# Carrying a super-tile's last projection and its sum of squares into the next super-tile, in a recurrent state-space layer

## The chip, the cores and the metric

The kernel runs on one core of one Trainium2 chip. The metric is the device time of one launch in microseconds (us); lower is better. The engines are TensorE (PE in the profile, with its weight loads as PEld), VectorE (DVE), ScalarE (ACT), GpSimd (POOL) and SyncE (SP), which here only issues DMAs.

## The reference, cut to what matters

```python
x = u                                       # (4, 1024, 128), 4096 tokens
xn = layernorm(x)
proj = xn @ in_proj_w.T                     # z, x, B, C, dt, theta, lambda; 32 heads of 64
B, C = rope(rms(B) + B_bias), rope(rms(C) + C_bias)      # per head, angles = cumsum(theta)
h = a_t * h + g_t * Bx_t + b_t * Bx_(t-1)   # state per head, scanned over the tokens
y = einsum(h, C) + D * x
y = y * silu(z)                             # 2048 features a token
y = y * rsqrt(mean(y * y) + eps) * norm_w
out = u + (y @ out_proj_w.T) * silu(fp8_ffn(xn))
```

The mean of squares runs over all 2048 features of a token, so it is known only when all heads are done. As it is one factor a token, the kernel projects the unscaled y and multiplies the result with the factor afterwards.

## The kernel before, in words

A first part (`prepare`) normalises the tokens, makes decays and tables, and stores them in DRAM; it lasts to about 137 us. The second part (`units`) is the rest. It works in 8 super-tiles `t` of 512 tokens (4 chunks of 128), and in each of them in 8 groups `q` of 4 heads (two pairs). One (t, q) is called a unit here; there are 64. A sequence has 1024 tokens, so `begins(t)` is true of even t and `ends(t)` of odd t; a super-tile that ends a sequence leaves out the last state update.

Each engine runs a list written out by hand, in which work for unit q, q+1 and q+2 is interleaved; semaphores hold the engines together, and `at(per, t, k)` is the count that a wait asks for.

- DVE in a unit: two products `part` a rotation (`rotation`, L1220), of B and C with sines and cosines, eight a unit and one of them ahead of `angles` (L1194); the state updates (L1269, L1279), `x_scaled` (L1204, from the two banks R[0] and R[1]), `scores` (M, L1238), `yT` = y * silu(z) (L1311), `b_decayed` (bw, L1230).
- POOL in a unit: `sums` (L1412) adds two `part` into `rot`, four times; `c_decayed` (ce, L1421); the running sum `sqa` of the squares of yT (L1465, in q = 0 L1458).
- ACT in a unit: `rounding`, `decays` (E, L1353), silu of z (sz, L1388), `sines`, `squares` (sq, L1358).
- PE in a unit: `angles`, the state products (L1111), `exponents` (L1051, into bank Dp), `scores` (L1062), `x_by_token` (L1036, two halves, into R[0] and R[1]), `project` (L1076, the output projection of the unit before, 16 matmuls into the bank Op, which one matmul of zeros opens, L1071), z (L1137), y (L1143, L1149, L1159, banks Yp[0] and Yp[1]), then B by token (L1042) and the first exponents and scores of the next unit.

At the end of a super-tile PE runs the projection of the last unit (`project(t, 7, range(CS))`, L1175) and then the sums of squares (L1180: 8 small matmuls of `sqa` with ones into Dp), and only then the next super-tile's angles and state products. DVE takes the sums in `norm_start` (L1244) of the next super-tile's unit 0, between its first rotation product and its `angles`; ACT takes the root (L1364), DVE the reciprocal (`norm_seeded`, L1249), POOL refines it in four small operations (`norm_refined`, L1427 to L1433, between `c_decayed` and the second of the four `sums`), ACT scales Op into `so` (`normalised`, L1372, four pieces, last in its unit 0), and POOL multiplies with the gate and adds the residual at the end of unit 1 (`finished`). PE waits for `ssq_taken`, which `norm_start` raises, before its state products of unit 0, and for `acc_done`, which `normalised` raises, before the first projection of the new super-tile in unit 1.

Of the kernel before, what the change touches and what calls it, by code (L numbers as in the profile page):

```python
# [27 lines left out]
P = 128  # L28
# [5 lines left out]
CS = 4  # L34
# [788 lines left out]
def units(nc, K, u, scratch, cum_stored, out):  # L823

    xn_d, tc_d, bc_d, cum_d, cumt_d, gate_d, ecum_d = scratch
    with ExitStack() as ctx:
# [196 lines left out]
        def _(pe):  # L1023
# [43 lines left out]
            def project(t, q, chunks):  # L1067

                if q == 0 and chunks[0] == 0:
                    pe.wait_ge(acc_done, at(1, t, 0))  # L1070
                    nc.tensor.matmul(Op[:], K["zeros_bf"][0:MASK_ROWS, :], K["cum"][0:MASK_ROWS, 0, 0, :], start=True, stop=False, skip_group_check=True)  # L1071
                pe.wait_ge(yt_ready, at(T2, t, 2 * q + 2))
                for c in chunks:
                    k = slice(c * P, c * P + P)
                    for p in range(2):
                        last = nc.tensor.matmul(Op[:, k], yT[:, p, k], K["w_o"][:, (2 * q + p) * P:(2 * q + p + 1) * P],  # L1076
                                                start=False, stop=q == NQ - 1 and c == CS - 1 and p == 1,
                                                skip_group_check=True)
                if chunks[-1] == CS - 1:
                    last.then_inc(out_ready, 1)  # L1080


            pe.wait_ge(xn_loaded, 16)
# [10 lines left out]
            for t in range(NS):  # L1094
                for q in range(NQ):
# [6 lines left out]
                    if live(t, q + 2):  # L1102
                        angles(t, q + 2)
                    if q == 0:
                        pe.wait_ge(ssq_taken, at(1, t, 0))

                    pe.wait_ge(bw_ready, at(T2, t, 2 * q + 2))
# [9 lines left out]
                    scores(t, q, 1)  # L1117
                    exponents(t, q, 3)
                    if live(t, q + 1):
                        if q == NQ - 1:  # L1120
                            pe.wait_ge(xn_loaded, (t + 2) * 16)
                        if live(t, q + 2):
                            pe.wait_ge(turned, at(T1, t, q + 3))
                        x_by_token(t, q + 1, 0)
                    if q > 0:
                        project(t, q - 1, (0, 1))
                    pe.wait_ge(hch, at(T8, t, 8 * q + 8))
                    if live(t, q + 1):
                        x_by_token(t, q + 1, 1)
                    if q > 0:  # L1130
                        project(t, q - 1, (2, 3))
                    for p in range(2):
# [4 lines left out]
                        nc.tensor.matmul(R[p][:], w, xns[:, t % 2, :], start=True, stop=True).then_inc(z_ready, 1)  # L1137

                    for p in range(2):
                        pe.wait_ge(m_ready, at(T4, t, 4 * q + 2 * p + 2))  # L1140
# [33 lines left out]
                    exponents(t, q + 1, 1)  # L1174
                project(t, NQ - 1, range(CS))  # L1175

                pe.wait_ge(sqa_ready, at(T2, t, T2))
                pe.wait_ge(e_ready, at(T4, t, T4 + 2 if live(t, NQ) else T4))
                for c in range(CS):
                    last = nc.tensor.matmul(Dp[:, c:c + 1], sqa[:, c * P:c * P + P], K["ones"][:, 0:1],  # L1180
                                            start=True, stop=True)
                last.then_inc(ssq_ready, 1)

        @block.vector
        def _(dve):
# [54 lines left out]
            def norm_start(t):  # L1240

                dve.wait_ge(ssq_ready, at(1, t, 1))
                dve.wait_ge(norm_ready, t)
                nc.vector.tensor_scalar(nrm[:, 0, :], Dp[:, 0:CS], 1.0 / DI, EPS, ALU.mult, ALU.add).then_inc(ssq_taken, 1)  # L1244

# [15 lines left out]
            for t in range(NS):  # L1261
# [21 lines left out]
                for q in range(NQ):  # L1283
                    tn = t if q < NQ - 1 else t + 1
                    if live(t, q + 1):
                        rotation(t, q + 1, 0, 0, 0)
                    if q == 0 and t > 0:
                        norm_start(t - 1)
                    if live(t, q + 2):
# [3 lines left out]
                    if live(t, q + 1):  # L1293
                        rotation(t, q + 1, 0, 0, 1)
                        x_scaled(t, q + 1, tn, 0)
                        x_scaled(t, q + 1, tn, 1)
                    scores(t, q, 2)
                    scores(t, q, 3)
                    if q == 0 and t > 0:
                        norm_seeded(t - 1)  # L1300
                    if live(t, q + 1):
                        for p, w in ((1, 0), (0, 1), (1, 1)):
                            rotation(t, q + 1, p, w, 0)
                            rotation(t, q + 1, p, w, 1)

                    for p in range(2):
# [21 lines left out]
        def _(act):  # L1328
# [48 lines left out]
            for t in range(NS):  # L1377
                for q in range(NQ):
                    if live(t, q + 2):
                        rounding(t, q + 2)  # L1380
                    decays(t, q, 2)
                    decays(t, q, 3)
                    if q == 0 and t > 0:
                        root(t - 1)
# [11 lines left out]
                    squares(t, q, 1)  # L1396
                    if q == 0 and t > 0:
                        normalised(t - 1)
            root(NS - 1)
# [3 lines left out]
        def _(pool):  # L1403
# [42 lines left out]
            for t in range(NS):  # L1446
                for q in range(NQ):
                    if live(t, q + 1):
                        sums(t, q + 1, 0)
                    c_decayed(t, q)  # L1450
                    if q == 0 and t > 0:
                        norm_refined(t - 1)
                    if live(t, q + 1):
                        for k in range(1, 4):
                            sums(t, q + 1, k)
                    if q == 0:
                        pool.wait_ge(sq_ready, at(T2, t, 2))
                        nc.gpsimd.tensor_tensor(sqa[:], sq[:, 0, :], sq[:, 1, :], ALU.add).then_inc(sqa_ready, 1)  # L1458
                        pool.wait_ge(sqa_ready, at(T2, t, 1))
                        pool.sem_inc(sqa_ready, 1)  # L1460
                        continue
                    for p in range(2):
# [44 lines left out]
```

## Time and profile before

| | |
|---|---|
| median of 3 runs | 1283.85 us (1281.26 to 1285.37) |
| the profiled execution | 1283.93 us, span 1282.2 us |
| DVE busy | 1195.0 us, 93% of the span |
| PE busy | 1124.5 us, 88% |
| ACT busy, POOL busy | 737.9 us and 736.5 us |
| mean granted TensorE clock | 0.967 of full |

Busy time is counted per engine, so they overlap. An engine's idle time is put down to the instruction that released it. Timeline rows give the start in the span, the length, and in brackets the idle time ahead.

### The profile page before, as it was taken

How to read it: one execution, taken by the hardware profiler on the slowest of the kernel's cores; microseconds unless marked ns; L12 is line 12 of the kernel's file. 1: busy time of each engine (PE TensorE's matmuls, PEld its weight loads, DVE VectorE, ACT ScalarE, POOL GpSimd, SP SyncE). 2: the span in 40 equal slices, each digit the busy share in tenths (PEclk: the TensorE clock that was granted, in tenths of full speed). 3: DMA queues.
4: the chain of work that ended last, by engine and by line, in shares of the span. 5: the costliest groups of instructions: out<-in, count | busy, mean ns of one | idle time of the engine just before them, and what ended most of it. 6: DMA issues, size and time to landing. Idle time of an engine off the chain costs nothing. (4 is left out here: it accounts for less than half of the span.)

```text
span 1282.2 us, 30215 instructions
## 1 busy us (share of the span) xinstructions
PE 1124.5 (88%) x11410; PEld 819.9 (64%) x11410; DVE 1195.0 (93%) x1925; ACT 737.9 (58%) x1133; POOL 736.5 (57%) x588
## 2 busy tenths in 40 slices
PE   3876499998999999999999899989999899999996
PEld 3752366766666666666666666666667666666665
DVE  7998599998999899998999899999999899989994
ACT  4776155555655565556655655556555656556553
POOL 4000166666666666565766576657666576666664
PEclk9876699999999999999999999999999999999998
DMA  8534464345544355445544454346444455434441
GB/s 187 185 99 123 111 139 102 97 93 123 126 117 97 74 146 113 100 104 108 112 107 103 114 130 102 88 96 150 108 109 91 107 122 117 100 88 90 106 98 26
DMA packets 88468, 141.26 MB, mean 110 GB/s; under 512 B 16099, under 2 KB 35268, under 8 KB 88004
## 3 DMA queue, kind: packets, MB, share of 16 engines
q1 hardware_dynamic: 88323, 139.33, 46.4%
q8 instruction: 91, 1.49, 0.5%
q14 instruction: 54, 0.43, 0.1%
HBM read 57.89 MB, written 12.58 MB: 55 GB/s over the span
## 5 line engine op out<-in xcount | busy, mean ns | idle before, releaser
L1412 POOL TENSOR_TENSOR rot<-part 128x512 f32<-128x512 f32 x256 | 375.5, 1468 | 507.7 <-DVE part L1220 507.1
L1220 DVE SCALAR_TENSOR_TENSOR part<-bcs,k_prmT,k_trig 128x512 f32<-128x512 f32 x512 | 502.0, 1028 | 22.1 <-DMA bcs<-bc_t 12.4
L1353 ACT ACTIVATE E<-d 128x512 f32<-128x512 f32 x256 | 151.8, 593 | 192.5 <-PE d L1051 192.5
L1062 PE MATMUL s<-rot 64*128 64x128 f32 x2048 | 150.4, 286 | 26.6 <-POOL rot L1412 26.3
L1388 ACT ACTIVATE sz<-r 128x512 f32<-128x512 f32 x128 | 76.5, 597 | 165.5 <-PE r L1137 165.4
L1062 PEld LDWEIGHTS s<-rot 64*128 64x128 f32 x2048 | 127.6, 189 | 64.6 <-issue 64.4
L1238 DVE TENSOR_TENSOR M<-s,E 128x512 f32<-128x512 f32 x256 | 163.7, 679 | 2.4 <-PE s L1062 1.8
L1421 POOL TENSOR_TENSOR ce<-rot,eb 128x512 f32<-128x512 f32 x128 | 160.1, 1271 | 0.0
L1465 POOL TENSOR_TENSOR sqa<-sqa,sq 128x512 f32<-128x512 f32 x112 | 142.5, 1272 | 16.2 <-ACT sq L1358 7.8
L1036 PE MATMUL r<-k_w_zx,xns 128*128 128x256 f32 x512 | 131.8, 383 | 12.5 <-DMA xns<-xn_t 12.5
L1149 PE MATMUL y<-M,xk 128*64 128x128 f32 x2048 | 140.1, 279 | 0.0
L1076 PEld LDWEIGHTS o<-k_w_o,yT 128*128 128x128 f32 x1024 | 132.3, 191 | 11.5 <-DVE yT L1311 5.0
L1076 PE MATMUL o<-k_w_o,yT 128*128 128x128 f32 x1024 | 134.3, 276 | 2.7 <-DVE yT L1311 2.7
L1137 PE MATMUL r<-xns,k_w_zx 128*128 128x512 f32 x256 | 129.1, 617 | 5.1 <-DVE xc L1204 4.2
L1149 PEld LDWEIGHTS y<-M,xk 128*64 128x64 f32 x2048 | 109.2, 136 | 21.5 <-issue 21.5
L1358 ACT ACTIVATE sq<-yT 128x512 f32<-128x512 f32 x128 | 80.0, 625 | 61.0 <-DVE yT L1311 61.0
L1031 PE MATMUL r<-tcs,k_w_th 128*128 128x512 f32 x124 | 71.8, 662 | 46.9 <-DVE bw L1230 46.9
L1036 PEld LDWEIGHTS r<-k_w_zx,xns 128*128 128x128 f32 x512 | 93.7, 193 | 21.9 <-DMA xns<-xn_t 12.7
L1051 PE MATMUL d<-k_cum,k_pick 111*128 111x512 bf16 x256 | 99.8, 390 | 0.0
L1111 PEld LDWEIGHTS r<-xk,bw 128*64 128x64 f32 x1792 | 59.3, 141 | 52.6 <-DVE bw L1230 42.9
L1204 DVE TENSOR_TENSOR xk<-r,k_kk 128x512 f32<-128x512 f32 x128 | 87.5, 683 | 4.3 <-PE r L1036 4.3
L1311 DVE TENSOR_TENSOR yT<-y,sz 128x512 f32<-128x512 f32 x128 | 81.7, 677 | 6.3 <-PE y L1159 6.3
(243 smaller groups left out, 1671.1 us busy)
## 6 DMA issues: line engine op xcount, KB each, us to landing
k_trig<-k_tri SPq DMA_DIRECT2D x512, 128.0 KB, 2.4
eb<-ecum_rows SPq DMA_DIRECT2D x128, 256.0 KB, 4.7
bcs<-bc_t SPq DMA_DIRECT2D x16, 256.0 KB, 3.9
bcs<-bc_t SPq DMA_DIRECT2D x32, 128.0 KB, 3.9
a_big<-in_L_attn_u SPq DMA_DIRECT2D x4, 512.0 KB, 6.3
xn_t<-a_xnT SPq DMA_DIRECT2D x1, 2048.0 KB, 10.7
tc_t<-a_tcT SPq DMA_DIRECT2D x1, 2048.0 KB, 15.9
bc_t<-a_tmp SPq DMA_DIRECT2D x1, 2048.0 KB, 8.5
```

The source lines that it names most:

```text
L1036: last = nc.tensor.matmul(R[i][:, 256 * c:256 * c + 256], xns[:, (t + q // NQ) % 2, (2 * i + c) * P:(2 * i + c + 1) * P], K["w_zx"][:, DI ...
L1051: nc.tensor.matmul(Dp[:], K["pick"][:, head * P:head * P + P], K["cum"][0:D_ROWS, q % 2, h, :], start=True, stop=True).then_inc(d_ready, 1)
L1062: last = nc.tensor.matmul(Sp[j][:, k], rot[rows, q % 2, p, 0, k], rot[rows, q % 2, p, 1, k], start=True, stop=True)
L1076: last = nc.tensor.matmul(Op[:, k], yT[:, p, k], K["w_o"][:, (2 * q + p) * P:(2 * q + p + 1) * P], start=False, stop=q == NQ - 1 and c == ...
L1137: nc.tensor.matmul(R[p][:], w, xns[:, t % 2, :], start=True, stop=True).then_inc(z_ready, 1)
L1149: nc.tensor.matmul(Yp[p][m:m + 64, k], xk[:, par, c, 128 * p + m:128 * p + m + 64], M[:, 2 * p + j, k], start=False, stop=c == 0 and begin ...
L1220: nc.vector.scalar_tensor_tensor(out=part[:, 2 * p + f, :], in0=bcs[:, (t + q // NQ) % 2, 2 * w + f, :], scalar=col, in1=trig[:, p, 1 - f, ...
L1238: nc.vector.tensor_tensor(M[:, h, :], Sp[h % 2][:], E[:, h % 2, :], ALU.mult).then_inc(m_ready, 1)
L1353: nc.scalar.activation(E[:, h % 2, :], Dp[:], ACT.Exp).then_inc(e_ready, 1)
L1412: nc.gpsimd.tensor_tensor(rot[:, q % 2, p, w, :], part[:, 2 * p, :], part[:, 2 * p + 1, :], ALU.add).then_inc(rot_ready, 1)
L1421: nc.gpsimd.tensor_tensor(ce[:, p, :], rot[:, q % 2, p, 1, :], eb[:, p, :], ALU.mult).then_inc(ce_ready, 1)
L1465: nc.gpsimd.tensor_tensor(sqa[:], sqa[:], sq[:, p, :], ALU.add).then_inc(sqa_ready, 1)
```

## The change

The last projection of super-tile t-1 is issued inside unit 0 of super-tile t, in the same two halves that other units use, and the 8 small matmuls of the sum of squares become a function `square_sums`, called in unit 0 behind the exponents and ahead of `x_by_token`. They write into the bank Yp[0] and no longer into Dp. PE's wait for `ssq_taken` moves from ahead of the state products to ahead of the y matmuls. On DVE `norm_start` moves from ahead of `angles` to between the two halves of `x_scaled`, and `norm_seeded` from behind the M products to behind the next rotation. On POOL the four refining operations move from the middle of unit 0 to its end. On ACT `normalised` moves from the end of unit 0 into unit 1, behind its two exponentials. The projection of unit 0, issued in unit 1, is no longer split: all 16 matmuls and the zeros come behind both halves of `x_by_token`. The number and shape of all operations stay the same.

```diff
--- before.py
+++ after.py
@@ -1066,6 +1066,7 @@
 
             def project(t, q, chunks):
 
+                t, q = (t, q) if q >= 0 else (t - 1, NQ - 1)
                 if q == 0 and chunks[0] == 0:
                     pe.wait_ge(acc_done, at(1, t, 0))
                     nc.tensor.matmul(Op[:], K["zeros_bf"][0:MASK_ROWS, :], K["cum"][0:MASK_ROWS, 0, 0, :], start=True, stop=False, skip_group_check=True)
@@ -1079,6 +1080,14 @@
                 if chunks[-1] == CS - 1:
                     last.then_inc(out_ready, 1)
 
+            def square_sums(t):
+
+                pe.wait_ge(yt_ready, at(T2, t, T2))
+                pe.wait_ge(sqa_ready, at(T2, t, T2))
+                for c in range(CS):
+                    last = nc.tensor.matmul(Yp[0][:, c:c + 1], sqa[:, c * P:c * P + P], K["ones"][:, 0:1],
+                                            start=True, stop=True)
+                last.then_inc(ssq_ready, 1)
 
             pe.wait_ge(xn_loaded, 16)
             for i in range(2):
@@ -1101,9 +1110,6 @@
                         pe.wait_ge(tc_loaded, 16)
                     if live(t, q + 2):
                         angles(t, q + 2)
-                    if q == 0:
-                        pe.wait_ge(ssq_taken, at(1, t, 0))
-
                     pe.wait_ge(bw_ready, at(T2, t, 2 * q + 2))
                     for c in range(CS - 1 if ends(t) else CS):
                         for p in range(2):
@@ -1116,19 +1122,21 @@
                     exponents(t, q, 2)
                     scores(t, q, 1)
                     exponents(t, q, 3)
+                    if q == 0 and t > 0:
+                        square_sums(t - 1)
                     if live(t, q + 1):
                         if q == NQ - 1:
                             pe.wait_ge(xn_loaded, (t + 2) * 16)
                         if live(t, q + 2):
                             pe.wait_ge(turned, at(T1, t, q + 3))
                         x_by_token(t, q + 1, 0)
-                    if q > 0:
+                    if t + q > 0 and q != 1:
                         project(t, q - 1, (0, 1))
                     pe.wait_ge(hch, at(T8, t, 8 * q + 8))
                     if live(t, q + 1):
                         x_by_token(t, q + 1, 1)
-                    if q > 0:
-                        project(t, q - 1, (2, 3))
+                    if t + q > 0:
+                        project(t, q - 1, (2, 3) if q != 1 else range(CS))
                     for p in range(2):
 
                         if live(t, q + 1):
@@ -1136,6 +1144,8 @@
                         w = K["w_zx"][:, (2 * q + p) * P:(2 * q + p + 1) * P]
                         nc.tensor.matmul(R[p][:], w, xns[:, t % 2, :], start=True, stop=True).then_inc(z_ready, 1)
 
+                    if q == 0:
+                        pe.wait_ge(ssq_taken, at(1, t, 0))
                     for p in range(2):
                         pe.wait_ge(m_ready, at(T4, t, 4 * q + 2 * p + 2))
                         pe.wait_ge(yt_ready, at(T2, t, 2 * q - 1 + p))
@@ -1172,14 +1182,8 @@
                     exponents(t, q + 1, 0)
                     scores(t, q + 1, 0)
                     exponents(t, q + 1, 1)
-                project(t, NQ - 1, range(CS))
-
-                pe.wait_ge(sqa_ready, at(T2, t, T2))
-                pe.wait_ge(e_ready, at(T4, t, T4 + 2 if live(t, NQ) else T4))
-                for c in range(CS):
-                    last = nc.tensor.matmul(Dp[:, c:c + 1], sqa[:, c * P:c * P + P], K["ones"][:, 0:1],
-                                            start=True, stop=True)
-                last.then_inc(ssq_ready, 1)
+            project(NS - 1, NQ - 1, range(CS))
+            square_sums(NS - 1)
 
         @block.vector
         def _(dve):
@@ -1241,7 +1245,7 @@
 
                 dve.wait_ge(ssq_ready, at(1, t, 1))
                 dve.wait_ge(norm_ready, t)
-                nc.vector.tensor_scalar(nrm[:, 0, :], Dp[:, 0:CS], 1.0 / DI, EPS, ALU.mult, ALU.add).then_inc(ssq_taken, 1)
+                nc.vector.tensor_scalar(nrm[:, 0, :], Yp[0][:, 0:CS], 1.0 / DI, EPS, ALU.mult, ALU.add).then_inc(ssq_taken, 1)
 
             def norm_seeded(t):
 
@@ -1284,8 +1288,6 @@
                     tn = t if q < NQ - 1 else t + 1
                     if live(t, q + 1):
                         rotation(t, q + 1, 0, 0, 0)
-                    if q == 0 and t > 0:
-                        norm_start(t - 1)
                     if live(t, q + 2):
                         angles(t, q + 2)
                     for c in range(CS):
@@ -1293,15 +1295,17 @@
                     if live(t, q + 1):
                         rotation(t, q + 1, 0, 0, 1)
                         x_scaled(t, q + 1, tn, 0)
+                        if q == 0 and t > 0:
+                            norm_start(t - 1)
                         x_scaled(t, q + 1, tn, 1)
                     scores(t, q, 2)
                     scores(t, q, 3)
-                    if q == 0 and t > 0:
-                        norm_seeded(t - 1)
                     if live(t, q + 1):
                         for p, w in ((1, 0), (0, 1), (1, 1)):
                             rotation(t, q + 1, p, w, 0)
                             rotation(t, q + 1, p, w, 1)
+                            if q == 0 and t > 0 and (p, w) == (1, 0):
+                                norm_seeded(t - 1)
 
                     for p in range(2):
                         dve.wait_ge(sz_ready, at(T2, t, 2 * q + p + 1))
@@ -1380,6 +1384,8 @@
                         rounding(t, q + 2)
                     decays(t, q, 2)
                     decays(t, q, 3)
+                    if q == 1 and t > 0:
+                        normalised(t - 1)
                     if q == 0 and t > 0:
                         root(t - 1)
                     for p in range(2):
@@ -1394,8 +1400,6 @@
                     if live(t, q + 1):
                         decays(t, q + 1, 1)
                     squares(t, q, 1)
-                    if q == 0 and t > 0:
-                        normalised(t - 1)
             root(NS - 1)
             normalised(NS - 1)
 
@@ -1448,8 +1452,6 @@
                     if live(t, q + 1):
                         sums(t, q + 1, 0)
                     c_decayed(t, q)
-                    if q == 0 and t > 0:
-                        norm_refined(t - 1)
                     if live(t, q + 1):
                         for k in range(1, 4):
                             sums(t, q + 1, k)
@@ -1458,6 +1460,8 @@
                         nc.gpsimd.tensor_tensor(sqa[:], sq[:, 0, :], sq[:, 1, :], ALU.add).then_inc(sqa_ready, 1)
                         pool.wait_ge(sqa_ready, at(T2, t, 1))
                         pool.sem_inc(sqa_ready, 1)
+                        if t > 0:
+                            norm_refined(t - 1)
                         continue
                     for p in range(2):
                         pool.wait_ge(sq_ready, at(T2, t, 2 * q + p + 1))
```

## Rows read from the trace of the kernel before

**Rows 1.** The page: DVE's busy share in 40 slices of the span.
```profile
DVE  7998599998999899998999899999999899989994
```
**Rows 2.** Waits of DVE over the whole span: us in total, times, longest.
```profile
DVE ang L1194 <- ACT rnd L1338: 11.4, 9, 1.5
DVE part L1220 <- POOL rot L1412: 9.2, 7, 1.3
...
DVE xk L1204 <- PE r L1036: 4.3, 11, 0.9
```
**Rows 3.** DVE's timeline, the yT products of five units.
```profile
413.04 1.28 DVE L1311 TENSOR_TENSOR yT<-y,sz 128x512 f32<-128x512 f32 x2
430.06 1.28 DVE L1311 TENSOR_TENSOR yT<-y,sz 128x512 f32<-128x512 f32 x2
450.05 1.27 DVE L1311 TENSOR_TENSOR yT<-y,sz 128x512 f32<-128x512 f32 x2
...
554.93 1.27 DVE L1311 TENSOR_TENSOR yT<-y,sz 128x512 f32<-128x512 f32 x2
572.20 1.27 DVE L1311 TENSOR_TENSOR yT<-y,sz 128x512 f32<-128x512 f32 x2
```
**Rows 4.** DVE's timeline in unit 0 of super-tile 3.
```profile
577.45 0.16 DVE L1244 TENSOR_SCALAR nrm<-d 128x4 f32<-128x4 f32 x1 [0.59 <-PE d L1180]
579.14 0.69 DVE L1194 SCALAR_TENSOR_TENSOR ang<-rnd,r 128x512 f32<-128x512 f32 x1 [1.52 <-ACT rnd L1338]
...
589.61 2.40 DVE L1220 SCALAR_TENSOR_TENSOR part<-bcs,k_prmT,k_trig 128x512 f32<-128x512 f32 x2 [1.31 <-POOL rot L1412]
```
**Rows 5.** DVE by line, 554.93 to 572.20, then 572.20 to 591.93: busy, mean ns.
```profile
L1220 DVE SCALAR_TENSOR_TENSOR part<-bcs,k_prmT,k_trig 128x512 f32<-128x512 f32 x9 | 9.8, 1127 | 0.0
L1220 DVE SCALAR_TENSOR_TENSOR part<-bcs,k_prmT,k_trig 128x512 f32<-128x512 f32 x9 | 8.7, 1002 | 1.3 <-POOL rot L1412 1.3
```
**Rows 6.** PE's timeline, unit 7 of super-tile 2 and what follows it.
```profile
560.63 1.03 PE L1036 MATMUL r<-k_w_zx,xns 128*128 128x256 f32 x4
...
562.39 1.03 PE L1036 MATMUL r<-k_w_zx,xns 128*128 128x256 f32 x4
...
569.15 0.89 PE L1159 MATMUL y<-ce,hs 64*64 64x128 f32 x24
...
571.88 1.16 PE L1062 MATMUL s<-rot 64*128 64x128 f32 x16 [0.60 <-POOL rot L1412]
...
573.53 2.05 PE L1076 MATMUL o<-k_w_o,yT 128*128 128x128 f32 x16 [0.17 <-DVE yT L1311]
576.36 1.05 PE L1180 MATMUL d<-k_ones,sqa 128*128 128x1 f32 x8 [0.78 <-POOL sqa L1465]
577.27 1.11 PE L1031 MATMUL r<-tcs,k_w_th 128*128 128x512 f32 x2
```
**Rows 7.** DVE's timeline, unit 7 of super-tile 2, second half of x_scaled.
```profile
563.70 0.68 DVE L1204 TENSOR_TENSOR xk<-r,k_kk 128x512 f32<-128x512 f32 x1
```
**Rows 8.** POOL's timeline, unit 0 of super-tile 3, first and last refining operation.
```profile
585.71 0.65 POOL L1427 TENSOR_TENSOR tch<-nrm 128x4 f32<-128x4 f32 x1
...
587.76 0.58 POOL L1433 TENSOR_TENSOR nrm<-nrm,tch 128x4 f32<-128x4 f32 x1
```
**Rows 9.** DVE's timeline, unit 1 of super-tile 2, second half of x_scaled.
```profile
458.80 0.69 DVE L1204 TENSOR_TENSOR xk<-r,k_kk 128x512 f32<-128x512 f32 x1 [0.24 <-PE r L1036]
```
**Rows 10.** ACT's timeline, end of unit 0 and unit 1 of super-tile 2.
```profile
452.29 1.13 ACT L1372 ACTIVATE so<-o,nrm 128x128 f32<-128x128 f32 x4
...
455.95 0.60 ACT L1353 ACTIVATE E<-d 128x512 f32<-128x512 f32 x1 [0.82 <-PE d L1051]
...
460.55 0.60 ACT L1388 ACTIVATE sz<-r 128x512 f32<-128x512 f32 x1 [2.69 <-PE r L1137]
```
**Rows 11.** POOL's timeline, end of unit 0 of super-tile 2.
```profile
452.47 1.28 POOL L1458 TENSOR_TENSOR sqa<-sq 128x512 f32<-128x512 f32 x1 [0.99 <-ACT sq L1358]
```
**Rows 12.** Windows, unit 1 of super-tile 4: busy us, then PE's granted clock.
```profile
733.00:737.00 4.00, 3.80 (x35) 2.17 (x35) 3.29 (x6) 2.34 (x7) 1.26 (x1) 0.57 0.91 209
```

## The prediction

> **What bounds the kernel now.** I first read the busy share of each engine by slices [rows 1]: from the slice where the second part starts, DVE is at nine tenths nearly everywhere. PE's share, 88%, is close, but PE waits in every unit for DVE or POOL (0.60 us before its scores in an ordinary unit [rows 6]), so DVE sets the pace. What can be gained is then DVE's idle time, and the list of DVE's waits shows where it is [rows 2]. Three entries matter: DVE waits for ACT's rounded angles (`ang`), for POOL's `rot` before a rotation product, and for `x_by_token` (`xk`). The counts of 9 and 7 point to the seven passages from one super-tile to the next.
>
> The timeline of one passage gives their sizes [rows 4]: 0.59, 1.52 and 1.31 us, 3.42 us together. The other six passages repeat these numbers within 0.02 us. The first is for the sums of squares (`nrm`), the second for the angles, the third for `rot`. The cause of the first two is PE's order: the projection (2.05 us) and the eight small matmuls (0.91 us from their start to that of the angles) stand between the last scores and the angles of the new super-tile, and the small ones wait another 0.78 us for POOL's `sqa` [rows 6]. The third comes from the four refining operations on POOL, from 585.71 to 588.34 us [rows 8], which sit ahead of the second `rot` sum; DVE can't overwrite the two `part` buffers before that sum is done.
>
> Idle time isn't yet what a passage costs, so I measured that too, as the distance from one unit's yT to the next [rows 3]. An ordinary unit takes 17.02 us in an odd super-tile (413.04 to 430.06) and 17.27 us in an even one (554.93 to 572.20), which has one more state step. Unit 0 of super-tile 2 takes 19.99 us (430.06 to 450.05), 2.72 over the even value. Unit 0 of super-tile 3 ends 19.73 us after 572.20, as its parts start at 589.61 and take 2.40 us less the overlap [rows 4], which is 2.71 over the odd value. So the excess is 2.7 us, not 3.4.
>
> **Where the other 0.7 us is.** The nine `part` products between two yT take 9.8 us in the ordinary unit and 8.7 us at the passage [rows 5]. They are slower when a large POOL addition runs beside them. At the passage POOL is busy with 128x4 operations instead, so four products run fast and DVE arrives early at the wait of 1.31 us. Moving the refining away takes away the wait, and gives back about 1.1 us to slower products, so it gains about 0.2 us once the two small DVE operations (0.2 us together, in both kernels) are counted. The Trainium skill (SBUF — State Buffer, "Who interferes with whom") has the rule for this: a DVE instruction with two SBUF inputs contends with a GpSimd instruction that reads SBUF, by a lock held for a whole instruction. By that rule, the trace agrees, 9.8 against 8.7 us; it speaks against this part of the change. Without it the sum would take all 3.42 us of a passage and end near 1258; with it, near 1267.
>
> **The change, part by part.**
>
> *Projection and sums off the passage.* PE goes straight from the last exponents to the angles of unit 0, waiting only for `bw` as it does in all other units. The 0.59 and 1.52 us go. Together with the refining, a passage falls to an ordinary unit plus what is put into it: 2.71 us minus that.
>
> *The eight small matmuls in unit 0.* They need `sqa` of the last unit. PE reaches them where it reaches `x_by_token` in an ordinary unit: 560.63, which is 577.90 one unit of 17.27 us later, and in the kernel before `sqa` was there by 576.3 (the matmuls started at 576.36 when it came [rows 6]). So they don't wait, with 1.5 us to spare. They push both halves of `x_by_token` 0.91 us back. In the ordinary unit the halves end at 561.66 and 563.42 [rows 6] and DVE takes the second at 563.70 [rows 7] and the first two products of 0.60 us earlier, at 562.50: 0.84 and 0.28 us to spare. So the first is 0.07 us late. The second is 0.63 us late, of which 0.07 has gone already and about 0.16 is covered by `norm_start`, now between the two: a new wait of 0.40 us. Price of a passage: 0.47 us, and 0.2 us for `norm_start` and `norm_seeded`, so 0.65 to 0.7 us. Between nothing and 0.9 us is possible; the shift is measured, so I take 0.65.
>
> *The rest of unit 0.* PE stays 0.91 us behind its ordinary place, DVE 0.65 us behind its own, so PE loses 0.26 us of slack. The y matmuls end 2.16 us before yT in the ordinary unit (570.04 against 572.20 [rows 3, 6]) and the 0.60 us wait before the scores takes up the lag; PE is on its ordinary place in unit 1. PE's wait for `ssq_taken` ahead of y is always met, since the second z before it needs the second half of `x_scaled`, which stands behind `norm_start`. ACT's root now waits for `norm_start` too, and silu of z stands behind the root; but silu waits for z anyway (2.69 us in unit 1 [rows 10]), and z is 0.9 us later here: hidden.
>
> *Unit 1.* The second half of `x_by_token` no longer stands behind the zeros and half of the projection. The wait of 0.24 us [rows 9] occurs in unit 1 of seven super-tiles as 0.24 to 0.26 us, and once, in super-tile 4, as 0.69 us; it is part of the 4.3 us of [rows 2]. It goes, in all eight: 2.0 us. The projection now needs `normalised` on ACT. That starts when ACT's second exponential ends, 456.55, and when POOL's refining is done: `sqa` ends at 453.75 [rows 11], four operations take 2.63 us [rows 8], 456.38. It takes 1.13 us [rows 10], so `acc_done` comes at 457.7, and PE ends `x_by_token` about then. Zeros and 16 matmuls take 2.05 and some 0.2 us, so z is 0.3 us later than before. Silu of z follows; its table load has 2.69 us of idle time behind it [rows 10], of which 1.13 is used. No cost, while `acc_done` is less than about 2 us later than this; beyond, it is one for one, seven times.
>
> *Ends.* The last super-tile has no next one, and its tail of projection, sums and output stays as it is. DMA issues don't move: no DMA waits for `ssq_taken` or `norm_ready`, and the output store waits for POOL's `finished`, still at the end of unit 1.
>
> **The sum.** 7 x (2.71 - 0.65) = 14.4 us, and 8 x 0.25 = 2.0 us: 16.4 us. The profiled execution took 1283.93 us, 0.08 above the median of 1283.85, so the scale is the same. 1283.9 - 16.4 = **1267.5 us**.
>
> **Rivals.**
> 1. *The whole idle time comes back* (10%). If the slower `part` products overlap waits that I don't see, a passage gains 3.42 us, 24 us in all, and with unit 1's 2 us the time is 1258. Against it: [rows 5]; ordinary units have the slow products every time.
> 2. *A new wait in the moved chain* (22%). The order of PE in units 0 and 1 is new, and a wait of about 1 us a passage more than I count, for `x_by_token` or for the scores behind a PE that doesn't catch up, or for the sines whose transfer then lands late, gives 7 us back: 1274.5. For it: 0.28 us was all the slack of the second half. Against it: the 2.16 us of slack ahead of yT.
> 3. *The time doesn't change* (4%). This needs the 2.35 us of a passage to be paid in unit 0 or 1 in full: 1280 to 1284.
> 4. *Slower* (4%). One mechanism does it: `normalised` stands in ACT's list ahead of silu of z, and PE's projection waits for it ahead of z and y. If POOL's refining came more than 2 us later than the 456.4 us worked out, z, y and yT would be late one for one; from 4.3 us on (2 us of slack and the 2.35 us gained) the kernel is slower, and with 6 us it would be 1296. For it: POOL gets there only after a `sqa` that waits for ACT's last square. Against it: POOL then idles until the next rotation in the kernel before, and 4 us is more than the four operations take.
>
> TensorE's clock is a smaller matter. In unit 1 of super-tile 4 the granted clock was 0.57, between the levels of 1.2 and 2.4 GHz, for 4 us after PE had waited [rows 12], and that unit's waits were longer. Whether it happens again is worth 1.5 us either way, and PE waits less afterwards.
>
> The likeliest case has 60%, with its own range of 1263 to 1272. The lower bound of the price in unit 0, nothing in place of 0.65 us, would give 1263, and a part of rival 1 lies below it; rival 2 is to be held, with a little beyond. So the range is 1261 to 1277, and it leaves out most of rival 1 and the last two. A measurement of this kernel can't tell 0.3%, 3.9 us, from no change. Faster by more than that is 92%, within it 4%, slower 4%.
>
> **What would show it.** In the waits of DVE, `nrm` is down to the one at the end, `ang` has lost its seven waits of 1.5 us and `part` those for `rot`. The distance between the yT before and after a passage is 17.7 us (odd) or 17.9 us (even) in place of 19.73 and 19.99. The nine `part` products there take 9.8 and not 8.7 us. A wait of 0.4 us for `x_by_token` shows in unit 0 and none in unit 1. I am wrong if a passage still takes over 18.5 us, or if unit 1 takes longer than 17.2 us; then ACT's `so` and PE's `o` of unit 1 are to be looked at first.

## The result, and the profile after

The changed kernel takes 1265.46 us in the median of its runs (1264.76 to 1270.63), against 1282.77 us (1281.26 to 1285.37) of the kernel before beside it. The ratio is 0.987, with an interval of 0.984 to 0.990. In a second comparison with more runs it was 1264.45 against 1283.39 us, ratio 0.986 (0.983 to 0.989). The gain is thus 17.3 us in one comparison and 18.9 in the other. Forecast were 1267.5 us, a gain of 16.4 us, and a range of 1261 to 1277.

The page of the changed kernel has DVE at nine tenths in every slice from the sixth to the last but one, where the kernel before had eight tenths in six of them [rows 1]:

```profile
DVE  7699599999999999999999999999999999999994
```

The waits of DVE over the whole span (us in total, times, longest), to be read against [rows 2]:

```profile
DVE nrm L1248 <- PE y L1088: 4.0, 1, 4.0
...
DVE xk L1208 <- PE r L1036: 3.1, 8, 0.5
...
DVE part L1224 <- DMA k_trig<-k_tri: 0.9, 3, 0.5
```

The entries for the rounded angles and for `rot` are gone, and the sums of squares are waited for once, at the very end. What is left of `x_by_token` has another place. DVE's timeline in unit 0 of super-tile 3, the counterpart of [rows 4]:

```profile
576.31 1.06 DVE L1224 SCALAR_TENSOR_TENSOR part<-bcs,k_prmT,k_trig 128x512 f32<-128x512 f32 x1
577.30 0.67 DVE L1198 SCALAR_TENSOR_TENSOR ang<-rnd,r 128x512 f32<-128x512 f32 x1
...
580.15 0.69 DVE L1208 TENSOR_TENSOR xk<-r,k_kk 128x512 f32<-128x512 f32 x1
...
581.36 0.15 DVE L1248 TENSOR_SCALAR nrm<-y 128x4 f32<-128x4 f32 x1
581.91 0.69 DVE L1208 TENSOR_TENSOR xk<-r,k_kk 128x512 f32<-128x512 f32 x1 [0.40 <-PE r L1036]
```

The angles follow the rotation product at once, and one wait of 0.40 us stands ahead of the second half of `x_scaled`. The distance between two yT around it is 590.39 - 572.72 = 17.67 us, where it was 19.73 us:

```profile
572.72 1.28 DVE L1315 TENSOR_TENSOR yT<-y,sz 128x512 f32<-128x512 f32 x2
...
590.39 1.27 DVE L1315 TENSOR_TENSOR yT<-y,sz 128x512 f32<-128x512 f32 x2
607.30 1.27 DVE L1315 TENSOR_TENSOR yT<-y,sz 128x512 f32<-128x512 f32 x2
```

I took this distance for all 63 pairs of neighbours in every kernel, since it is free of what happens in the first part; a table of it stands at the end of the experiments. The first part does scatter. In the profiled executions of all kernels the first yT comes either at 169 to 170 us or at 175 to 176 us; that of the changed kernel is one of the late ones (1270.63 us). In the three late ones DVE waits 8.9 or 9.0 us for ACT's `a_tmp` in the first part, in all others 2.4 us. The spread of the unprofiled runs, some 6 us between two clusters, is probably the same.

The nine part products of the passage, by line, to be read against [rows 5]:

```profile
L1224 DVE SCALAR_TENSOR_TENSOR part<-bcs,k_prmT,k_trig 128x512 f32<-128x512 f32 x9 | 9.7, 1115 | 0.0
```

They take 9.7 us where they took 8.7: a good part of the wait for `rot` came back as slower products.

### The profile page after: what moved, and what is told of

The parts are those of the page before. It is cut to its first block and busy times, and to the rows that moved or that the text cites. A ratio compares the mean times of both kernels' runs of the same rounds, so it can differ in the third digit from the quotient of the medians.

```text
span 1268.9 us, 30207 instructions
## 1 busy us (share of the span) xinstructions
PE 1122.5 (88%) x11410; PEld 822.3 (65%) x11410; DVE 1201.2 (95%) x1925; ACT 738.5 (58%) x1133; POOL 735.4 (58%) x588
## 5 line engine op out<-in xcount | busy, mean ns | idle before, releaser
L1416 POOL TENSOR_TENSOR rot<-part 128x512 f32<-128x512 f32 x256 | 382.6, 1495 | 494.2 <-DVE part L1224 493.0
L1224 DVE SCALAR_TENSOR_TENSOR part<-bcs,k_prmT,k_trig 128x512 f32<-128x512 f32 x512 | 509.8, 1043 | 13.5 <-DMA bcs<-bc_t 12.4
L1036 PE MATMUL r<-k_w_zx,xns 128*128 128x256 f32 x512 | 134.6, 387 | 12.7 <-DMA xns<-xn_t 12.2
L1145 PE MATMUL r<-xns,k_w_zx 128*128 128x512 f32 x256 | 126.5, 611 | 1.1 <-DVE xc L1208 0.7
L1153 PEld LDWEIGHTS y<-k_ident,xc 128*128 128x128 f32 x512 | 58.8, 140 | 44.7 <-issue 31.6
```

The lines of the kernel that those rows point to most:

```text
L1036: last = nc.tensor.matmul(R[i][:, 256 * c:256 * c + 256], xns[:, (t + q // NQ) % 2, (2 * i + c) * P:(2 * i + c + 1) * P], K["w_zx"][:, DI ...
L1224: nc.vector.scalar_tensor_tensor(out=part[:, 2 * p + f, :], in0=bcs[:, (t + q // NQ) % 2, 2 * w + f, :], scalar=col, in1=trig[:, p, 1 - f, ...
L1416: nc.gpsimd.tensor_tensor(rot[:, q % 2, p, w, :], part[:, 2 * p, :], part[:, 2 * p + 1, :], ALU.add).then_inc(rot_ready, 1)
```

## The experiments

**POOL's refining back in its old place.** In the changed kernel:

```diff
@@ DVE
                     scores(t, q, 3)
+                    if q == 0 and t > 0:
+                        norm_seeded(t - 1)
...
-                            if q == 0 and t > 0 and (p, w) == (1, 0):
-                                norm_seeded(t - 1)
@@ POOL
                     c_decayed(t, q)
+                    if q == 0 and t > 0:
+                        norm_refined(t - 1)
...
-                        if t > 0:
-                            norm_refined(t - 1)
```

> The changed kernel with one part undone: POOL's four refining operations stand again in the middle of unit 0 (behind c_decayed) and norm_seeded on DVE behind the M products. Theory (the lock between the part products and POOL's large additions gives most of the wait back): DVE waits 1.3 us for rot in each of seven unit 0, but the nine part products there fall from 9.7 to about 8.7 us, so a passage takes 17.9 instead of 17.68 us (odd), and the kernel is 1 to 3 us slower than the changed one. Rival (idle time counts in full): 1.3 us a passage, 9.2 us slower than the changed one, passages of 19.0 us.

Measured: 1265.92 us (1265.32 to 1271.21). DVE's waits have all seven of the old ones back:

```profile
DVE part L1224 <- POOL rot L1416: 9.2, 7, 1.3
```

and yet a passage grew from 17.68 to 18.03 us (odd) and from 17.90 to 18.26 us (even): 0.35 us for 1.31 us of new idle time, 2.5 us in all. The nine part products of the passage fall to 8.7 us (mean 999 ns), as said. The theory stands; its 0.2 us was a little low. The medians are only 0.5 us apart, which these runs can't tell from nothing: that 9.2 us didn't come back they do show, the 2.5 us rest on the passages. So about three quarters of DVE's idle time there stood in place of slower products.

**One of the two carried pieces put back.** First the 8 small matmuls at the end of the super-tile again, with the projection carried over:

```diff
-                    if q == 0 and t > 0:
-                        square_sums(t - 1)
...
                     exponents(t, q + 1, 1)
+                if t < NS - 1:
+                    square_sums(t)
```

> The changed kernel with the 8 small matmuls issued again at the end of the super-tile, into Yp[0]; the projection stays carried over. Theory (PE's wait for sqa, the last of the sum, is what holds up the passage, and the projection lies in its shadow): PE still reaches the angles some 1.5 us after DVE's first part product, DVE waits about 2 us for the rounded angles and the wait of 0.40 us goes; the kernel is 11 to 15 us slower than the changed one, near 1278. Rival (the projection of 2 us is what holds up the passage): near the changed kernel, within 4 us.

Measured: 1298.75 us (1297.92 to 1302.49), ratio to the kernel before 1.014 (1.012 to 1.015). That is 33 us over the changed kernel and 17 over the kernel before that ran beside it. Neither theory had that. PE's timeline at the passage into super-tile 3:

```profile
579.92 1.84 PE L1088 MATMUL y<-k_ones,sqa 128*128 128x1 f32 x8 [3.08 <-POOL sqa L1469]
581.62 2.05 PE L1031 MATMUL r<-tcs,k_w_th 128*128 128x512 f32 x2
583.60 1.55 PE L1117 MATMUL r<-xk,bw 128*64 128x64 f32 x24
```

and the windows around it: us of the window, then busy us of PE, PEld, DVE, ACT and POOL, PE's granted clock, the DMA share and GB/s:

```profile
578.00:581.00 3.00, 1.08 (x6) 1.11 (x6) 2.32 (x4) 0.02 (x1) 1.63 (x2) 0.53 0.63 136
581.00:585.00 4.00, 4.00 (x30) 2.46 (x30) 0.57 (x1) 0.69 (x1) 0.00 (x0) 0.50 0.00 0
585.00:590.00 5.00, 5.00 (x44) 4.34 (x41) 4.01 (x12) 3.28 (x5) 2.45 (x2) 1.00 0.00 0
```

With the projection gone from that place, TensorE is idle for 3.08 us while it waits for `sqa`. The granted clock was 1.00 from 575 to 578 us; it goes to 0.50, which is 1.2 GHz, until 585 us, and the angles take 2.05 and not 1.11 us. DVE waits 4.11 us for the rounded angles, in the other passages 3.3 to 4.1:

```profile
584.43 0.69 DVE L1198 SCALAR_TENSOR_TENSOR ang<-rnd,r 128x512 f32<-128x512 f32 x1 [4.11 <-ACT rnd L1342]
```

Second the counterpart, the projection back and the small matmuls carried over:

```diff
-                    if t + q > 0 and q != 1:
+                    if q > 1:
                         project(t, q - 1, (0, 1))
...
-                    if t + q > 0:
+                    if q > 0:
                         project(t, q - 1, (2, 3) if q != 1 else range(CS))
...
+                if t < NS - 1:
+                    project(t, NQ - 1, range(CS))
```

> The counterpart: the changed kernel with the whole last projection issued again at the end of the super-tile; the 8 small matmuls stay carried over. Theory (the projection lies in the shadow of the wait for sqa): angles come 1.15 us later than in the changed kernel, DVE waits 0.4 us for them and up to 0.7 us for the first half of x_by_token, the wait for the second goes; the kernel is 3 to 6 us slower than the changed one. Rival (the projection is what holds it up): 10 us or more slower.

Measured: 1272.38 us (1268.11 to 1274.96). Passages take 18.36 to 18.45 us (odd) and 18.61 to 18.69 us (even), 0.7 to 0.8 more than changed, 5.1 us in all; its profiled execution has a late first part, and a granted clock of 0.95 up to 590 us, where the passages are the slower ones. Its waits are the two that were forecast, the second a little longer than the 0.7 us:

```profile
578.90 0.69 DVE L1200 SCALAR_TENSOR_TENSOR ang<-rnd,r 128x512 f32<-128x512 f32 x1 [0.39 <-ACT rnd L1344]
...
582.56 0.69 DVE L1210 TENSOR_TENSOR xk<-r,k_kk 128x512 f32<-128x512 f32 x1 [0.84 <-PE r L1036]
```

So the small matmuls, 0.9 us of PE, are what had to be carried over; the projection's 2 us lay mostly in the shadow of their wait for `sqa`.

**The gap filled.** To part the clock from the wait, the kernel with the small matmuls back got the projection's 16 matmuls once more, into Yp[0], ahead of them (8 calls in the code, x16 in the trace); they are extra work that is overwritten.

```diff
+                if t < NS - 1:
+                    pe.wait_ge(yt_ready, at(T2, t, T2))
+                    for c in range(CS):
+                        for p in range(2):
+                            nc.tensor.matmul(Yp[0][:, c * P:c * P + P], yT[:, p, c * P:c * P + P], K["w_o"][:, p * P:p * P + P], start=True, stop=True)
+                    square_sums(t)
```

> The kernel with the 8 small matmuls back at the end of the super-tile, and 8 extra matmuls of the projection's shape into Yp[0] ahead of them, whose result is overwritten, so that TensorE isn't idle while it waits for sqa. Theory (the run without them was 33 us slower than the changed kernel since TensorE's granted clock fell after 3.08 us of idle time): the clock stays at 1.0, the angles take 1.1 and not 2.05 us, DVE waits about 2.2 us for the rounded angles and not 4.1, passages take about 20.0 us; the kernel is near 1281. Rival (the place of the small matmuls costs that much by itself): passages stay over 21.5 us.

Measured: 1279.08 us (1277.78 to 1288.72), 20 us less than without the extra matmuls. Passages take 19.96 us (odd) and 20.2 us (even), against 21.8 to 23.3 us without: 17 us over the seven passages. PE's and DVE's rows of the passage:

```profile
571.43 2.05 PE L1187 MATMUL y<-k_w_o,yT 128*128 128x128 f32 x16 [0.17 <-DVE yT L1320]
574.35 1.02 PE L1088 MATMUL y<-k_ones,sqa 128*128 128x1 f32 x8 [0.87 <-POOL sqa L1474]
575.24 1.10 PE L1031 MATMUL r<-tcs,k_w_th 128*128 128x512 f32 x2
```

```profile
577.10 0.69 DVE L1203 SCALAR_TENSOR_TENSOR ang<-rnd,r 128x512 f32<-128x512 f32 x1 [2.35 <-ACT rnd L1347]
```

The granted clock is 1.00 from 571 to 580 us, and the wait is the one forecast for the order alone. By the passages, of the 33 us of the run before 16 were the order and 17 what follows from leaving TensorE idle, its clock.

**Unit 1: the projection split again.**

```diff
-                    if t + q > 0 and q != 1:
+                    if t + q > 0:
                         project(t, q - 1, (0, 1))
...
-                        project(t, q - 1, (2, 3) if q != 1 else range(CS))
+                        project(t, q - 1, (2, 3))
```

> The changed kernel with the projection of unit 0 split in halves again in unit 1, so that the wait for acc_done stands ahead of the second half of x_by_token; all else as changed. Theory (acc_done comes 1 us and more after the first half of x_by_token, and the second half has little slack): DVE waits 1.2 to 1.8 us for the second half in unit 1 of seven super-tiles, 8 to 13 us slower than the changed kernel. Rival (PE's place has slack enough): 2 us slower, the 0.24 us wait back in eight units.

Measured: 1277.49 us (1271.95 to 1279.46). Unit 1 takes 17.96 us (odd) and 18.19 us (even), 1.25 to 1.27 us more than the usual value of the changed kernel, 9 us in seven super-tiles. Six of its ten runs lie above 1277 us and the others near 1272.7; the first are probably those with a late first part. PE waits 0.86 us for `acc_done` and DVE then 1.29 us for the second half:

```profile
593.34 0.39 PE L1072 MATMUL o<-k_cum,k_zeros_bf 85*128 85x512 bf16 x1 [0.86 <-ACT so L1376]
```

```profile
595.52 0.69 DVE L1208 TENSOR_TENSOR xk<-r,k_kk 128x512 f32<-128x512 f32 x1 [1.29 <-PE r L1036]
```

The unsplit projection of unit 1 is thus what lets `normalised` move there.

**The same step alone, in the kernel before.** In unit 1 both halves of `x_by_token` first, then all of the projection.

```diff
-                    if q > 0:
+                    if q > 1:
                         project(t, q - 1, (0, 1))
...
-                        project(t, q - 1, (2, 3))
+                        project(t, q - 1, (2, 3) if q > 1 else range(CS))
```

> The kernel before with one part of the change alone: in unit 1 the zeros and all 16 projection matmuls come behind both halves of x_by_token. Theory (the eight waits of 0.25 us in unit 1 come from that order alone): unit 1 falls by 0.25 us, 2 us in all, under what the runs can tell, but clear in DVE's waits. Rival (they come from what the passage leaves late): the waits stay.

Measured: 1284.84 us (1278.87 to 1287.03), no difference that the runs can tell (ratio 0.998 to 1.002). In the profile unit 1 falls from 16.94 to 16.69 us (odd) and from 17.16 to 16.94 us (even), and DVE's waits of 0.24 to 0.26 us there are gone. The theory holds for six of the eight. In super-tiles 3 and 4 unit 1 took 17.69 and 17.93 us; the angles took 1.95 and 2.08 us there, after 1.43 and 1.44 us in which PE was idle. The first of the two:

```profile
590.88 1.95 PE L1031 MATMUL r<-tcs,k_w_th 128*128 128x512 f32 x2 [1.43 <-DVE bw L1230]
```

**How late `acc_done` may be.** Extra activations in ACT's list ahead of `so`, in unit 1 of seven super-tiles, 3 of them and then 8; what they write is read by nothing.

```diff
                 act.wait_ge(o_ready, t)
+                for i in range(3 if t < NS - 1 else 0):
+                    nc.scalar.activation(pad[:, i, :], Op[:], ACT.Copy, scale=nrm[:, 1, 0:1])
```

> The changed kernel with 3 extra activations of 128x512 (about 1.7 us together) in ACT's list ahead of the four that make acc_done, in unit 1 of seven super-tiles; they write a buffer that nothing reads. Theory (rival 4 of the prediction: acc_done may come about 2 us later at no cost): no change beyond 0.5 us a passage. Rival (no slack is left behind acc_done): 1.7 us a passage, 12 us slower than the changed kernel.

Measured: 1273.73 us (1271.89 to 1278.25). DVE's timeline in units 1 and 2 of super-tile 3:

```profile
603.26 1.29 DVE L1316 TENSOR_TENSOR yT<-y,sz 128x512 f32<-128x512 f32 x2 [0.42 <-issue]
...
606.49 0.69 DVE L1243 TENSOR_TENSOR M<-s,E 128x512 f32<-128x512 f32 x1 [0.15 <-ACT E L1358]
607.10 1.77 DVE L1225 SCALAR_TENSOR_TENSOR part<-bcs,k_prmT,k_trig 128x512 f32<-128x512 f32 x1
```

Unit 1 takes 17.18 and not 16.69 us (17.20 and not 16.94 in even super-tiles), and unit 2 takes 18.27 and not 17.31 us. For 1.7 us of delay 1.2 to 1.45 us are paid, so the theory of no cost is wrong. In the changed kernel the last y matmuls end at 606.01 us and yT follows at 607.30 us: 1.3 us (1.5 in super-tile 2), where I had counted with about 2. That accounts for the longer unit 1. And the lateness goes on into unit 2: squares and `sqa` come later, so that its first rotation product runs into POOL's additions and takes 1.77 us (1.07 in the changed kernel):

```profile
605.64 2.68 POOL L1472 TENSOR_TENSOR sqa<-sqa,sq 128x512 f32<-128x512 f32 x2 [1.46 <-ACT sq L1363]
```

> The same with 8 extra activations, about 4.4 us. Theory (2 us are free, the rest is one for one): 2.4 us a passage, 17 us slower than the changed kernel, that is about where the kernel before is. If TensorE's clock falls while it waits for acc_done, more. Rival (all is hidden, other slack takes it): within 5 us of the changed kernel.

Measured: 1307.06 us (1306.38 to 1307.92), 42 us over the changed kernel. PE's timeline:

```profile
608.44 0.58 PE L1073 MATMUL o<-k_cum,k_zeros_bf 85*128 85x512 bf16 x1 [4.41 <-ACT so L1379]
608.81 3.44 PE L1078 MATMUL o<-k_w_o,yT 128*128 128x128 f32 x16
```

The extra activations put `so` off by 4.55 us. Unit 1 grows by 4.8 to 6.0 us, unit 2 by 0.96 us as in the run before, 6.0 us a passage on average. PE is idle for 4.41 us, and the projection behind it takes 3.44 and not 1.95 us: the granted clock was 0.57 from 608 to 612 us. The forecast had named this ("more").

**Unit 0: the projection unsplit as well.**

```diff
-                    if t + q > 0 and q != 1:
+                    if q > 1:
                         project(t, q - 1, (0, 1))
...
-                        project(t, q - 1, (2, 3) if q != 1 else range(CS))
+                        project(t, q - 1, (2, 3) if q > 1 else range(CS))
```

> The changed kernel with the carried projection also unsplit: in unit 0, as in unit 1, both halves of x_by_token come first and then all 16 projection matmuls. Theory (the 0.40 us wait for x_by_token in unit 0 is all that the 8 small matmuls cost, and comes from the half projection between the two halves): it vanishes, passages take 17.3 (odd) and 17.5 us (even), 2.8 us less than the changed kernel in all. Rival (the second half then waits for the state updates, or z comes later and something behind it is late): no change or slower.

Measured: 1263.39 us (1260.24 to 1267.94). Passages take 17.18 us (odd) and 17.41 us (even), 0.49 less than changed, and the 0.40 us wait is gone. The rest is `norm_start`, whose time the wait had covered in part: the second half of `x_scaled` now starts 0.07 us after it and no longer 0.55 us. As the scatter of the first part is larger than the 3.4 us that this makes in seven passages, it ran once more beside the changed kernel.

> The changed kernel itself, for a comparison on one chip with the next two: 1264 to 1267 us.

> The changed kernel with the projection in unit 0 unsplit, once more, beside the changed kernel itself. Theory: 7 x 0.49 us = 3.4 us faster, by the passages of its first run. Rival: what the passages gain is lost in the scatter of the first part, no difference between the medians.

Measured: 1264.45 us (1263.41 to 1265.51) for the changed kernel and 1260.25 us (1259.68 to 1261.41) for this one; no run of the one lies among those of the other. 7 x 0.49 = 3.4 us of the 4.2 are the passages. Beside the kernel before its ratio is 0.983 (0.980 to 0.985), so it is faster than both.

The distances between yT in us, odd and then even super-tiles, for these kernels. Passages are given as measured, unit 1 by its usual value; single units that took longer are in the text:

| | passage (unit 0) | unit 1 |
|---|---|---|
| before | 19.74, 19.99 | 16.94, 17.17 |
| changed | 17.67, 17.90 | 16.69, 16.94 |
| refining back | 18.03, 18.26 | 16.69, 16.95 |
| small matmuls back | 21.8 to 23.3 | 16.7, 16.95 |
| the same, gap filled | 19.96, 20.2 | 16.68, 16.94 |
| projection back | 18.4, 18.65 | 16.7, 16.95 |
| unit 1 split | 17.67, 17.90 | 17.96, 18.19 |
| acc_done 1.7 us later | 17.67, 17.90 | 17.18, 17.20 |
| unit 0 unsplit | 17.18, 17.41 | 16.75, 16.95 |

## Why the prediction was right

*The passage.* Forecast were 17.7 and 17.9 us; measured 17.67 and 17.90. The waits of 0.59 and 1.52 us are gone, as said, and the seven passages give 14.5 us (14.4 forecast). The experiments show both halves of the reason: it was PE's wait for `sqa` that held the passage up, and with the small matmuls alone carried over 5 of the 14.5 us are missing, with the projection alone all of them and more.

*The third wait.* Read as idle time it was 1.31 us, 9.2 us in all. It was counted at 0.2 us a passage and was worth 0.35 us. The step behind this, comparing the busy time of the same nine products in two windows, is also what kept the forecast from 1258 us. Rival 1 is out.

*The new wait.* 0.40 us for the second half of `x_by_token` was forecast from 0.28 us of slack and a shift of 0.91 us, and the row has 0.40. Its cause is shown by the run with unit 0 unsplit.

*Unit 1.* 8 x 0.25 = 2.0 us were forecast, which is too much. In the profile of the changed kernel unit 1 takes 16.68 us in super-tiles 1 and 7, but 16.91 and 17.02 in 3 and 5. In 5 DVE now waits 0.24 us for the sines' transfer ahead of the first rotation product, and in 3 the same product starts 0.19 us later than it does in 7, for which the profile names no wait. Seven of them together gave 1.0 us; the eighth, in super-tile 4, is the one whose clock was low before. I had left such a wait out of the sum and named it in rival 2.

*The rest.* From first to last yT the profiled executions differ by 18.8 us. 14.5 are passages and 1.0 unit 1. Of the other 3.3 us, 3.2 are two units of the kernel before, unit 1 of super-tile 4 and unit 6 of super-tile 7. They took 18.67 and 17.86 us, and 16.95 and 16.40 us after. The granted clock was low in both: 0.57 in the first [rows 12] and 0.58 from 1241 to 1245 us in the second. For the second PE stands idle for 1.46 us ahead of the state products in both kernels, before and after:

```profile
1241.52 1.49 PE L1111 MATMUL r<-xk,bw 128*64 128x64 f32 x24 [1.46 <-DVE bw L1230]
```

```profile
1229.61 0.92 PE L1117 MATMUL r<-xk,bw 128*64 128x64 f32 x24 [1.46 <-DVE bw L1234]
```

The change doesn't touch this place, and over the thirteen profiled executions that unit took 17.7 to 18.0 us in six and 16.4 us in seven; one and the same kernel, that with unit 0 unsplit, had 17.86 us in its first profiled execution and 16.40 in its second. These 1.5 us are chance. Unit 1 fell short of its forecast by about half, and the clock gave some 3 us; the prediction named it, at 1.5 us either way, but had it in no term of the sum. So the total came out as near as it did in part by luck; the passages did not.

*What was wrong without showing in the time* is the bound given for unit 1 and used in rival 4: "`acc_done` is less than about 2 us later than this" costs nothing, "beyond, it is one for one". 1.7 us cost up to 1.45 us and 4.55 us cost 6.0 on average. The slack ahead of yT had been read in an ordinary unit of an even super-tile (2.16 us), while unit 1 has 1.3 us in an odd one, and neither the later `sqa` (0.96 us in unit 2) nor the clock was in the rule. With 2.3 us gained a passage, the kernel would be slower than before from 2.6 to 2.8 us on, not from 4.3; this is an estimate from the slack of 1.3 to 1.5 us, the 0.96 us and the first of the two runs. The four refining operations, counted at 2.63 us, take 1.57 us in their new place (rows below), but that changed nothing: `so` starts when ACT's second exponential is done, at 596.56 us, and the refining had ended at 595.83.

## What to carry to other kernels

Before an idle time is counted as gain, the busy time of the same instructions in a stretch without it has to be compared: here 1.31 us of idle time was worth 0.35, since the products ran faster while the small POOL operations that caused the wait stood in place of a large addition. The distance from one recurring instruction to the next gives the net of both at once, and is free of scatter elsewhere. When work is moved off a place where an engine waits, ask what it covered: without the projection, TensorE's idle time at the same place turned a gain into a loss.

## What the runs showed of the hardware

An idle TensorE lost half its clock. After 3.08 us of idle time the granted clock went from 1.00 to 0.50, and in all seven passages the angles behind it took 2.05 us; in the run with the gap filled, with 0.87 us of idle time, they took 1.1 us. The cost was 1.6 to 3.1 us a passage, beside 2.3 us for the order. Shorter gaps are followed by slow angles sometimes. In the kernel before PE is idle for 1.43 us ahead of the angles of unit 1, in seven super-tiles; in one of them (super-tile 4, [rows 12]) the angles took 2.08 us, and in the kernel before with unit 1 unsplit they were slow in super-tiles 3 and 4. With POOL's refining back the same gap stands in seven places, and none was slow. A gap of 0.86 us stands ahead of the angles of unit 6 in every kernel, and in the changed one it was followed by slow angles once, in super-tile 2, a unit of 18.53 us:

```profile
538.93 1.73 PE L1031 MATMUL r<-tcs,k_w_th 128*128 128x512 f32 x2 [0.87 <-DVE bw L1234]
```

Over all thirteen profiled executions the angles in the second part were slow behind 7 of 7 gaps of 3.08 us, 3 of 21 of 1.43 us, 5 of 91 of 0.86 us, and behind none of some 600 of 0.77 us. Ahead of unit 1 the changed kernel has a gap of 0.77 us, and no unit 1 of it had a slow clock. With 3 of 21 that isn't enough to show that the shorter gap is why, and what else decides isn't shown.

The four small operations of POOL take as long as DVE's products let them. In the kernel before, in the seven passages, they ran beside rotation products and took 0.56 to 0.66 us each; in their new place the last three take 0.2 us, but for one of 0.57 in super-tile 5:

```profile
594.26 0.73 POOL L1431 TENSOR_TENSOR tch<-nrm 128x4 f32<-128x4 f32 x1 [0.18 <-POOLq L1462]
595.07 0.20 POOL L1433 TENSOR_TENSOR tch<-tch,nrm 128x4 f32<-128x4 f32 x1
...
595.63 0.20 POOL L1437 TENSOR_TENSOR nrm<-nrm,tch 128x4 f32<-128x4 f32 x1
```

The first still ran beside one, from 594.18 us on. The Trainium skill (SBUF — State Buffer, "Who interferes with whom") lets such a pair contend by a lock held for the whole instruction. The traces agree on both sides: POOL's operation of 0.2 us takes 0.73 beside a product of 0.75 and ends with it, and DVE's product at 607.10 us in the delayed kernel takes 1.77 us, where the second of POOL's two additions from 605.64 us lasts to 608.32.
